# Other PSUM banks for second down projections, rows and norms of a two-layer attention and expert kernel

## The reference

```
x = x + mlstm(layernorm(x), ctx, ctx, Wi, bi, Wf, bf, ln_scale)     # 16 heads of 32
x = x + experts(layernorm(x), gate_weight, gate_up, down, groups)   # 8 groups, hidden 192 each
x = x + ssm_mixer(ctx, ctx, layernorm(x), kernel, D)
x = x + moe(layernorm(x), ...)                                      # 7 routed experts, 1 shared
```

## Time and profile before

| | us |
|---|---|
| median of 3 runs | 2082.75 |
| lowest, highest | 2080.5, 2086.22 |
| the profiled execution | 2090.85 |
| its span, first to last instruction | 2089.1 |
| PE, DVE, ACT, POOL busy in it | 1910.4, 1394.5, 803.8, 639.8 |
| mean granted clock of PE | 0.965 of full |

### The profile page before, as it was taken

One profiled execution on the slowest core, in us unless ns is written; L12 is line 12 of the kernel. 1 busy time (PEld: TensorE's weight loads), 2 busy tenths in 40 slices (PEclk: granted clock), 3 DMA queues, 4 the chain that ended last, 5 costly groups with the idle time before them and its releaser, 6 DMA issues. The chain is left out here.

```text
span 2089.1 us, 35151 instructions
## 1 busy us (share of the span) xinstructions
PE 1910.4 (91%) x13798; PEld 1624.2 (78%) x13798; DVE 1394.5 (67%) x2817; ACT 803.8 (38%) x1484; POOL 639.8 (31%) x507
## 2 busy tenths in 40 slices
PE   4689999999999999999999997999988988988997
PEld 2368888888888878999999996677676777767886
DVE  5677877787788875655555553588866857783654
ACT  3445445454555542322222221454444443232332
POOL 1333333333333331000000000576755620002563
PEclk9699999999999999999999998999999988998999
DMA  4211212211111115222222222644433444324674
GB/s 120 73 52 66 77 61 73 81 67 67 62 62 62 62 42 181 71 101 101 92 101 101 101 72 89 231 114 141 159 106 122 143 157 143 109 94 142 163 184 64
DMA packets 111750, 214.64 MB, mean 103 GB/s; under 512 B 14242, under 2 KB 34786, under 8 KB 110562
## 3 DMA queue, kind: packets, MB, share of 16 engines
q1 hardware_dynamic: 104194, 195.30, 27.8%
q0 software_dynamic: 7392, 17.11, 4.0%
HBM read 136.11 MB, written 76.34 MB: 102 GB/s over the span
## 5 line engine op out<-in xcount | busy, mean ns | idle before, releaser
L1372 PE MATMUL psum<-kv,toep 128*128 128x288 f32 x1280 | 328.3, 419 | 43.1 <-ACT yx L1420 27.1
L1372 PEld LDWEIGHTS psum<-kv,toep 128*128 128x128 f32 x1280 | 249.3, 196 | 119.5 <-ACT yx L1420 32.7
L168 PE MATMUL psum<-xn_t_h,w_gate_h 128*128 128x256 f32 x768 | 233.2, 304 | 1.3 <-DVE th L292 1.3
L170 PE MATMUL psum<-xn_t_h,w_gate_l 128*128 128x256 f32 x768 | 217.6, 283 | 0.0
L169 PE MATMUL psum<-xn_t_l,w_gate_h 128*128 128x256 f32 x768 | 217.6, 283 | 0.0
L168 PE MATMUL psum<-xn_t_h,w_up_h 128*128 128x256 f32 x768 | 217.5, 283 | 0.0
L169 PE MATMUL psum<-xn_t_l,w_up_h 128*128 128x256 f32 x768 | 217.5, 283 | 0.0
L170 PE MATMUL psum<-xn_t_h,w_up_l 128*128 128x256 f32 x768 | 216.6, 282 | 0.0
L1038 POOL TENSOR_SCALAR_AFFINE_SELECT operands<-operands 128x512 f32<-128x512 f32 x128 | 93.9, 734 | 354.9 <-ACT operands L781 354.9
L275 ACT ACTIVATE th<-psum 128x256 f32<-128x256 f32 x192 | 73.8, 384 | 308.8 <-PE psum L170 308.1
L161 POOL TENSOR_TENSOR rstd<-rstd,minus_half 128x2 f32<-128x2 f32 x48 | 35.0, 730 | 503.6 <-DVE rstd L157 503.6
(11 more groups left out here) (305 smaller groups left out, 4733.9 us busy)
## 6 DMA issues: line engine op xcount, KB each, us to landing
toep<-ssm_padded_scratch SPq DMA_DIRECT2D x64, 256.0 KB, 3.6
kx<-in_ctx_pairs SPq DMA_DIRECT2D x32, 384.0 KB, 4.2
x_scratch<-x_all SPq DMA_DIRECT2D x21, 512.0 KB, 2.8
x_all<-in_x SPq DMA_DIRECT2D x16, 512.0 KB, 3.8
operands<-in_ctx_t SPq DMA_DIRECT2D x16, 512.0 KB, 4.8
xn_t_scratch<-xn_t_h SPq DMA_DIRECT2D x16, 512.0 KB, 2.7
xn_t_scratch<-xn_t_l SPq DMA_DIRECT2D x16, 512.0 KB, 3.6
xn_t_h<-xn_t_scratch SPq DMA_DIRECT2D x16, 512.0 KB, 3.7
```

Of the source, the lines that this page charges most:

```text
L168: pe.run.matmul(out, lhs[0], rhs[0], start=first, stop=False)
L170: return pe.run.matmul(out, lhs[1], rhs[0], start=False, stop=last)
L1372: ins = pe.run.matmul(out, w[:, (o - k) * P:(o - k + 1) * P], pairs, start=(k == 0), stop=(k == o))
```

## The change

Three stages get other banks: `rows` bank 5 in place of 6, `norms` bank 7 in place of 6 (but for batch 0, where it stays in 6), and the second `down` stage of every batch bank 6 in place of 5 (for the last two batches it was there already). Nothing else is edited; the order of the stages and all instructions stay, and only the waits for banks change with the plan.

```diff
                     elif name in ("gates", "norms", "rows"):
-                        banks.plan((name, b), 6)
+                        banks.plan((name, b), {"gates": 6, "norms": 7 if b else 6, "rows": 5}[name])
...
                     elif name == "down":
-                        banks.plan((name, b, 0, at[0]), 5 + at[0] * (b >= B - 2))
+                        banks.plan((name, b, 0, at[0]), 5 + at[0])
```

## The result

The changed kernel takes 2067.23 us (median of 4 runs, 2064.7 to 2069.57) against 2084.47 us (4 runs, 2080.5 to 2086.22). The ratio is 0.9914, 95% interval 0.9896 to 0.9933: 17.9 us less (14 to 22). Measured again on two chips, with the kernel before beside it each time, it gave 0.9904 (0.9887 to 0.9920) and 0.9903 (0.9888 to 0.9918). Forecast were 19.3 us less and 2063.4. The kernel before has a fourth run here, which moves its median from 2082.75 to 2084.47; 19.3 less than that is 2065.2.

A forecast was written before the change was run, and what follows sets the result against it. PE was taken to bound the kernel where attention and network overlap; 7.4 (down projection), 10.4 (norms), 0.4 and 1.1 (warm-up) sum to 19.3 us off 2082.75, giving 2063.4 us, range 2057 to 2071.

The forecast's parts named there:

- What bounds the kernel: From 163 to 747 us PE is busy 566 of 584 us; only time PE gets back counts.
- Second down projection: In bank 6 it no longer waits for DVE's first addition: 0.57 us in each of 13 repetitions, 7.4 us.
- The undisturbed hand-over of the last repetition: Score product to second down projection without decay rows: 0.21 us start to start, against 0.78 stalled.
- Norms: In bank 7 they no longer wait for ACT's copy of the rows: 0.80 us in 13 repetitions, 10.4 us.
- The unknown free hand-over: Last row product to norms without a stall: bounds 0.11 to 0.21 us, taken as 0.15.
- The cover of the decay products: After the norms, decay products would be due 0.2 us after ACT's copy of the rows: covered, but narrowly.
- Rival A: Decay products wait for ACT's copy, returning 0.1 to 0.8 us of each 0.80; at most 2073.8 us; chance 0.09.
- Warm-up: Norms' stalls in early batches: 0.4 us gained for batch 1, 1.1 for batch 2, nothing for batch 0.
- The sum: Whole kernel: 7.4 + 10.4 + 0.4 + 1.1 = 19.3 us less.
- The idle column: Profile's modelled PE idle times, the alternative to start-to-start: 13 x (0.52 + 0.68) = 15.5 us rather than 17.8.
- The clock, rival C: Changed PE pauses in the warm-up win or lose clock dips: 2058 or 2068 us; chance 0.06 beyond 2 us.

The follow-up runs named there:

- the five smaller edits: Five kernels making only some of the three bank moves, against the kernel before: ratios 0.9983, 0.9971, 0.9965, 0.9946 and 0.9934.
- `norms_only`: Only the norms move to bank 7 (batch 0 stays in 6), against the kernel before: ratio 0.9946, repetition 47.09 us.
- the doubled copy: ACT copies the rows twice, same result: added to the changed kernel 0.9932, to the kernel before 1.0080, both ratios to the kernel before.
- `down_only`: Only the second down projection moves, bank 5 to bank 6, against the kernel before: ratio 0.9983, repetition 47.73 us.

## Why the prediction was right, point by point

- **What bounds the kernel.** Right. PE's queue sets the repetition: with all three moves in place it is shorter by both terms, 1.33 against 0.575 + 0.745, and nothing on DVE or ACT took over. For the moves by themselves this does not hold; in four of the five smaller edits (all but `norms_only`) PE then waited for DVE's second addition, which took back part of the gain.
- **Second down projection.** 0.57 forecast, 0.57 measured (0.78 to 0.21 from start to start). The undisturbed hand-over of the last repetition was the right yardstick to 0.01 us.
- **Norms.** 0.80 forecast, 0.745 measured. The unknown free hand-over is 0.2, at the high end of the bounds and not at 0.15 as I chose. It is as long as the one in the earlier trace rows, so the small weights were no reason for the low end; what sets it was not tested. That is 0.7 us over 13 repetitions.
- **The cover of the decay products.** 0.2 forecast, about 0.3 in the trace and 0.29 by the doubled copy. Rival A did not occur; that the copy can hold the decay products is shown by the doubled one.
- **Warm-up.** The 1.5 us for batches 1 and 2 are not confirmed. Take 1.3 for the thirteenth repetition from what is gained up to the norms of batch 3, and 0.5 us are left in two profiles of the changed kernel and -1.8 in the first. The stalls are gone, but the same kernel reaches batch 3 at about 168.5 or 171 us. This term was mis-sized, or at least not measurable here.
- **The sum.** 17.8 forecast for the thirteen repetitions, 17.3 measured (13 x 1.33). In all 19.3 forecast, against 17.9 by the ratio of the result and 20.0 and 20.3 by the other two. That 19.3 comes so near is in part luck. The traces up to the second layer differ by 19.4 us in the two repeats, but 1.5 of that is a dip in the kernel before that the forecast did not count; it makes up for the warm-up and the norms. The idle column, which the prediction put at 15.5 (13 x 1.20 is 15.6), would have been short: in this trace it counts 0.51 and 0.68 where start to start says 0.57 and 0.745. The repetitions, said to repeat to 0.01 us, do so to 0.05 without the dip.
- **What the prediction did not see.** It argued each move in its final place and so was right that the rows find bank 5 free. It did not see that the three moves are not independent. Moving the rows alone still gains 0.27 us, since it parts them from the norms, but once the norms are in bank 7 it has no gain of its own: it clears the way that the second projection takes. This showed only when my expectations of the single moves, made on the same independence, failed. The total did not depend on it, because rows and second projection never shared a bank in the final plan.
- **The clock, rival C.** The prediction said that there was no clock to win from 163 to 747 us, and beside it that one repetition was 1.5 us longer, by a dip. That dip is there to win: the granted clock is 0.50 from 508 to 510 us in the kernel before, and no profile of the changed kernel dips in this stretch. Part of the difference between 17.3 us and the 20 us of the later measurements may be such dips in runs of the kernel before; those runs have no trace, so this stays open, as does the scatter of the second layer.

## What to carry to other kernels

Where several stages share few banks, price a move by its new neighbours on both sides: who empties the bank before it, and who comes to the bank after it, and how much of the matrix engine's work lies between. Move the whole chain in the plan and try its parts, since one good move can be paid back by the next neighbour. Measure a stall from start to start and look in the same trace for one hand-over that is free of it.

## What was not expected of the hardware

The granted clock of PE averaged 1.00 of full (2.4 GHz) from 175 to 725 us with idle times of 0.5 and 0.7 us in every repetition, with one dip to 0.50 (1.2 GHz) in the profile of the kernel before and none in `down_only`, which has pauses of 0.4 and 0.7. With the second pause lengthened to 1.3 us by the doubled copy, four of twelve repetitions dipped (mean 0.97 in the one shown) and cost 1.5 us each. Every one of these dips begins 1.6 to 2.1 us behind the start of the norms that had waited, though PE is busy by then. The profiles with no pause above 0.53 us had none. That the pause causes them is likely from this, but it rests on one trace of each kernel.
